# Second attention of a fused block: operand copies within SBUF, reciprocals at a head's last step, output stores ahead of expert weights, normalising on ScalarE

## The reference

```python
x = x + _L0_conv_ref(_gn(x), ...)                   # attention 0: softmax(q k^T * 32**-0.5 + rel_h + rel_w) v, projection
t = t + _L1_attn_ref(_ln_t(t), w_qkv, w_proj, b_proj)   # attention 1: softmax(q k^T / 384**0.5) v, projection
t = t + _L1_ffn_ref(_ln_t(t), ...)                  # top 2 of 8 experts, relu(x w1 + b1) w2 + b2

def _ln_t(v, eps=1e-05):
    m = jnp.mean(v, axis=-1, keepdims=True)
    s = jnp.var(v, axis=-1, keepdims=True)
    return (v - m) / jnp.sqrt(s + eps)
```

## Time and profile before

| | |
|---|---|
| Median of 3 runs (lowest to highest) | 999.45 us (996.57 to 999.99) |
| Profiled execution: its time and its span | 997.88 us, 996.1 us |
| PE, PEld busy | 879.5 us (88%), 675.1 us |
| DVE, ACT, POOL busy | 500.9 us, 353.8 us, 322.3 us |
| Chain of waits, share by engine | PE 41%, issue 7%, DVE 6%, POOL 4%, DMA 4%, SP's queue 4% |
| Attention 0's loop over heads, attention 1's loop | about 123 to 333 us, about 417 to 598 us |
| Closing stages | 339 to 360 us, 604 to 628 us |

### The profile page before, as it was taken

One profiled execution on the slowest core, in us unless ns is written; L12 is line 12 of the kernel. 1 busy time (PEld: TensorE's weight loads), 2 busy tenths in 40 slices (PEclk: granted clock), 3 DMA queues, 4 the chain that ended last, 5 costly groups with the idle time before them and its releaser, 6 DMA issues.

```text
span 996.1 us, 17661 instructions
## 1 busy us (share of the span) xinstructions
PE 879.5 (88%) x6045; PEld 675.1 (68%) x6046; DVE 500.9 (50%) x879; ACT 353.8 (36%) x582; POOL 322.3 (32%) x191
## 2 busy tenths in 40 slices
PE   4969699999999899999999998319999999999991
PEld 3447377677675444666666645319999999999991
DVE  5323666666663344777787725602442442442433
ACT  0112054454545322245455462303342342342330
POOL 0200057677677220166676760140000000000403
PEclk9989699999999999999999999559999999999996
DMA  8474823343334008535555370630652652643214
GB/s 288 96 166 124 289 84 86 100 136 101 106 111 159 13 0 207 142 118 150 191 175 181 121 255 14 232 119 32 238 202 68 245 176 93 230 167 118 87 39 135
DMA packets 77437, 139.21 MB, mean 140 GB/s; under 512 B 14264, under 2 KB 52152, under 8 KB 77392
## 3 DMA queue, kind: packets, MB, share of 16 engines
q1 hardware_dynamic: 66224, 120.62, 39.6%
q10 hardware_dynamic: 9120, 11.74, 3.5%
q0 software_dynamic: 2048, 6.29, 2.0%
HBM read 91.39 MB, written 43.55 MB: 135 GB/s over the span
## 4 chain that ended last, share of the span: by engine, by line
PE 41%; issue 7%; DVE 6%; POOL 4%; DMA 4%; SPq 4%; ACT 1%; ACTq 1%; DVEq 0%; POOLq 0%
PE ps L816 11%; PE ps L805 9%; PE ps L640 6%; PE ps L630 5%; PE ps L619 5%; SPq L362 2%; PE ps L736 2%; POOL xs L569 2%; POOL gy L576 2%; DVE w_lo L1016 1%; DMA xnT<-osb 1%; PE ps L605 1%; DVE mhalf L901 1%; POOL qf L521 1%; DMA heads<-parts 1%
## 5 line engine op out<-in xcount | busy, mean ns | idle before, releaser
L901 DVE TENSOR_REDUCE mhalf<-ps 128x1 f32<-128x512 f32 x384 | 242.5, 679 | 113.6 <-PE ps L619 111.6
L1079 ACT ACTIVATE prob<-ps 128x1024 f32<-128x1024 f32 x192 | 190.4, 1026 | 219.5 <-PE ps L640 95.7
L521 POOL TENSOR_TENSOR qf<-qf,prob 128x1024 f32<-128x1024 f32 x79 | 188.2, 2383 | 16.2 <-POOL qf L521 8.6
L805 PE MATMUL ps<-xT,w 128*128 128x128 f32 x1440 | 165.5, 276 | 1.6 <-issue 1.6
L805 PEld LDWEIGHTS ps<-xT,w 128*128 128x128 f32 x1440 | 164.9, 193 | 2.0 <-issue 2.0
L619 PE MATMUL ps<-km,qm 96*128 96x512 f32 x384 | 149.1, 463 | 7.8 <-DVE mhalf L901 6.8
L630 PE MATMUL ps<-qa,ka 97*128 97x512 f32 x384 | 146.8, 425 | 8.6 <-DMA qa<-row 8.6
L619 PEld LDWEIGHTS ps<-km,qm 96*128 96x128 f32 x384 | 113.3, 320 | 36.1 <-DVE mhalf L901 21.1
L1158 ACT ACTIVATE h_f<-ps,b1c 128x128 f32<-128x128 f32 x240 | 66.9, 377 | 149.0 <-PE ps L805 149.0
L640 PE MATMUL ps<-prob,va 128*32 128x256 f32 x1536 | 107.5, 385 | 0.0
L630 PEld LDWEIGHTS ps<-qa,ka 97*128 97x128 f32 x384 | 69.4, 191 | 54.5 <-issue 27.9
(11 more groups left out here) (128 smaller groups left out, 856.2 us busy)
## 6 DMA issues: line engine op xcount, KB each, us to landing
w<-in_w SPq DMA_DIRECT2D x24, 768.0 KB, 7.3
w_raw<-in_w SPq DMA_DIRECT2D x24, 768.0 KB, 11.9
heads<-parts SPq DMA_DIRECT2D x56, 256.0 KB, 4.6
qa<-heads SPq DMA_DIRECT2D x24, 256.0 KB, 3.6
ka<-heads SPq DMA_DIRECT2D x24, 256.0 KB, 3.7
qb<-heads SPq DMA_DIRECT2D x12, 512.0 KB, 4.5
xs<-zero SPq DMA_DIRECT2D x8, 768.0 KB, 3.8
qm<-heads SPq DMA_DIRECT2D x12, 384.0 KB, 3.7
```

The lines of the kernel that those rows point to most:

```text
L521: pool.tensor_tensor(acc[b], acc[b], prob[:, n % NP, :], ALU.add).then_inc(a_ok[L], 1)
L805: last = mm(ps[:, g, c % HG * P:(c % HG + 1) * P], w1[b][:, k, c * P:(c + 1) * P], xT[:, k, :], start=(k == 0), stop=(k == KT - 1))
L901: v.tensor_reduce(mhalf[:, b, qt, half:half + 1], ps[:, MAX_BANK[i], :], AX.X, ALU.max).then_inc(mx_ok[L], 1)
L1079: act.activation(prob[:, s % NP, :], ps[:, 3 + 2 * (s % 2):5 + 2 * (s % 2), :].rearrange("p a b -> p (a b)"), ACT.Exp).then_inc(p_ok[L], 1)
```

## The change

Five things change.

1. In attention 1, queries and keys are no longer written to DRAM and read back. SP copies them from `parts` to `qm`, `km`, `qa` and `ka`, one part of 32 partitions at a time, so `load_a` has six DMAs where it had four.
2. `invert_sums` runs all four pieces after step 7 of a head (after step 2 of the last head, which has no maxima).
3. In the closing stages ACT makes `tn` from a scale and a shift, DVE makes the shift (one column), the projection has five PSUM banks, and transposes and gate tiles come one step later.
4. `wproj` and the weights of attention 1 are loaded before the loop over heads.
5. Expert 0's weights are loaded after the last output stores, and after the last reads of `parts`.

```diff
@@ SP, per head
+                def held(h, name):
+                    g, m = h
+                    return f(parts[g * HD:(g + 1) * HD, bass.ds(m, 1), PART[name], :].rearrange("p m n -> p (m n)"))
...
                     wait(sp, st_ok[L], TT * (h - 1))
                     sp.sem_inc(a_free, 1)
-                    sp.dma_start(f(qa[b][0:2 * HD, :]), rows(h, "Q_LO", 2)).then_inc(ld_a[L][b], 16)
-                    sp.dma_start(f(qa[b][2 * HD:3 * HD, :]), rows(h, "Q_HI")).then_inc(ld_a[L][b], 16)
-                    sp.dma_start(f(ka[b][0:HD, :]), rows(h, "K_HI")).then_inc(ld_a[L][b], 16)
-                    sp.dma_start(f(ka[b][HD:3 * HD, :]), rows(h, "K_HI", 2)).then_inc(ld_a[L][b], 16)
                     if L == 0:
...
+                    else:
+                        at = at or (h % 4, h // 4)
+                        for i, (query, key) in enumerate((("Q_LO", "K_HI"), ("Q_HI", "K_HI"), ("Q_HI", "K_LO"))):
+                            sp.dma_start(f(qa[b][i * HD:(i + 1) * HD, :]), held(at, query)).then_inc(ld_a[L][b], 16)
+                            sp.dma_start(f(ka[b][i * HD:(i + 1) * HD, :]), held(at, key)).then_inc(ld_a[L][b], 16)
...
-                if L == 1:
+                if L == 0:
+                    for m in range(KT):
+                        store_qk(m)
+                else:
                     sp.wait_ge(pv_ok[0], TT * NH)
-                for m in range(KT):
-                    store_qk(m)
-                    if m == 0 and L == 1:
-                        sp.wait_ge(st_q[1][0], 16 * 8)
-                        first_heads()
+                    sp.wait_ge(split[1], 4)
+                    first_heads()
...
-                sp.wait_ge(st_q[L][1], 16 * 16)
                 load_row(0, 0)
                 load_m(2, 0)
                 load_row(1, 1)
                 load_m(3, 1)
+                if L == 0:
+                    sp.wait_ge(v_mm[0], TT)
+                    load_wqkv(1)
+                else:
+                    sp.wait_ge(pj_mm[0], TT)
+                    sp.wait_ge(split[1], 4 * KT)
+                sp.dma_start(wproj[:], ...).then_inc(ld_p[L], 16)
@@ PE, closing stage
-                        last = mm(ps[:, tt % 4, 0:C], oT[:, k, tt * P:(tt + 1) * P], wproj[:, k, :],
+                        last = mm(ps[:, tt % 5, 0:C], oT[:, k, tt * P:(tt + 1) * P], wproj[:, k, :],
...
-                for tt in range(TT + 3):
+                for tt in range(TT + 4):
                     if tt < TT:
-                        wait(pe, t_ok[L], tt - 3)
-                        project(tt, range(KT) if tt >= 4 else (2,)).then_inc(pj_mm[L], 1)
-                    if 2 <= tt < TT + 2:
-                        turn_stream(tt - 2)
-                    if tt >= 3 and L == 1:
-                        gate_tile(tt - 3)
+                        wait(pe, t_ok[L], tt - 4)
+                        project(tt, range(KT) if tt >= 5 else (2,)).then_inc(pj_mm[L], 1)
+                    if 3 <= tt < TT + 3:
+                        turn_stream(tt - 3)
+                    if tt >= 4 and L == 1:
+                        if tt == 4:
+                            pe.wait_ge(vs_ok[1], NH)
+                        gate_tile(tt - 4)
@@ DVE
-                        if 3 <= s < 7 and not first:
-                            invert_sums(h - 1, s - 3)
+                        if s == (TT - 1 if left else 2) and not first:
+                            for part in range(4):
+                                invert_sums(h - 1, part)
...
                         own(v.reciprocal(rstd[:, tt - 1:tt], sd[:, tt - 1:tt]))
-                        v.tensor_scalar(tn[:, tt - 1, :], t[:, tt - 1, :], mv[:, tt - 1, 0:1], rstd[:, tt - 1:tt],
-                                        ALU.subtract, ALU.mult).then_inc(tn_ok[L], 1)
+                        v.scalar_tensor_tensor(shift[:, tt - 1:tt], mv[:, tt - 1, 0:1], -1.0, rstd[:, tt - 1:tt],
+                                               ALU.mult, ALU.mult).then_inc(norm_ok[L], 1)
@@ ACT, closing stage
+                    if 1 <= tt < TT + 1:
+                        act.wait_ge(norm_ok[L], tt)
+                        act.activation(tn[:, tt - 1, :], t[:, tt - 1, :], ACT.Identity, bias=shift[:, tt - 1:tt],
+                                       scale=rstd[:, tt - 1:tt]).then_inc(tn_ok[L], 1)
```

More of the change, by code:

```diff
@@ L73, in build_program @@
         ps = ctx.enter_context(nc.psum_tensor("ps", [P, 8, HALF], F32))
-        heads_dram = [nc.dram_tensor(f"heads{L}", [NH, len(SLOTS[L]), HD, N], F32).ap() for L in range(2)]
+        heads_dram = nc.dram_tensor("heads", [NH, len(SLOTS), HD, N], F32).ap()
         xs_dram = nc.dram_tensor("xs", [FILLED * P, C], F32).ap()
@@ L250, in build_program @@
         sq_ok = [sem(f"sq_ok{L}") for L in L2]
+        norm_ok = [sem(f"norm_ok{L}") for L in L2]
         t_ok = [sem(f"t_ok{L}") for L in L2]
@@ L371, in load_m @@
+                def load_m(h, b, at=None):
                     wait(sp, sm_ok[L], 2 * TT * (h - 1))
                     sp.sem_inc(m_free, 1)
[L373 to L377, removed]
+                    if L == 0:
+                        sp.dma_start(f(qm[b][:]), rows(h, "Q_HI", 3)).then_inc(ld_m[L][b], 16)
+                        sp.dma_start(f(km[b][0:HD, :]), rows(h, "K_HI")).then_inc(ld_m[L][b], 16)
+                    else:
+                        at = at or (h % 4, h // 4)
+                        sp.dma_start(f(qm[b][0:HD, :]), held(at, "Q_HI")).then_inc(ld_m[L][b], 16)
+                        sp.dma_start(f(km[b][0:HD, :]), held(at, "K_HI")).then_inc(ld_m[L][b], 16)
@@ L444, in _ @@
                 load_m(3, 1)
+                if L == 0:
+                    sp.wait_ge(v_mm[0], TT)
+                    load_wqkv(1)
+                else:
+                    sp.wait_ge(pj_mm[0], TT)
+                    sp.wait_ge(split[1], 4 * KT)
+                sp.dma_start(wproj[:], a[f"wproj{L}"].rearrange("(k p) n -> p k n", p=P)).then_inc(ld_p[L], 16)
                 with sp.Fori(0, (NH - 4) // 4) as q:
@@ L476, in _ @@
                     store_quarter(sp, L, 1, 3, KT - 1, r)
+                if L == 1:
+                    for i in L2:
+                        sp.wait_ge(ld_m[1][i], 32 * NH // 2)
+                        sp.wait_ge(ld_a[1][i], 96 * NH // 2)
+                    load_expert(sp, 0, 0)
             sp.wait_ge(pj_mm[1], TT)
@@ L607, in _ @@
                     last.then_inc(qk_mm[L], 1)
-                n_m, n_a = (2, 5) if L == 0 else (2, 4)
+                n_m, n_a = (2, 5) if L == 0 else (2, 6)
                 kr = 96
@@ L744, in _ @@
                 pe.wait_ge(p_ok[L], TT * NH)
-                for tt in range(4):
+                for tt in range(5):
                     project(tt, (0, 1))
@@ L758, in gate_tile @@
                     for k in range(KT):
-                        last = mm(ps[:, 6, tt * NE:(tt + 1) * NE], xnT[:, k, tt * P:(tt + 1) * P], gate[:, k, :],
+                        last = mm(ps[:, 7, tt * NE:(tt + 1) * NE], xnT[:, k, tt * P:(tt + 1) * P], gate[:, k, :],
                                   start=(k == 0), stop=(k == KT - 1))
@@ L1104, in _ @@
                     store_quarter(act, L, 1, 3, KT - 1, r)
-                for tt in range(TT + 2):
+                for tt in range(TT + 3):
                     if tt < TT:
```

54 lines of the change are left out of this document (28 added, 26 removed).

## The result

The changed kernel takes **1000.6 us** in the median of 11 executions (998.85 to 1004.06), the kernel before 997.82 (11, 994.2 to 999.99): ratio 1.0041, 95% interval 1.0028 to 1.0054. The profiled execution took 998.85 us, its span is 997.0. Timed once more on another chip it took 1000.78 against 997.74, ratio 1.0045 (1.003 to 1.006). All ratios have their 95% interval behind them; they are given as recorded and are not the quotients of the two medians beside them (here 1.0028, and 1.003 the second time). So the difference is +2.8 and +3.0 us by the medians, +3.4 and +3.2 by the means, +4.1 and +4.5 by the ratios.

The account below looks back on a forecast made before the run. PE was taken as the bound, with 41% of the chain of waits. Terms +3.6 + 0.8 - 1.3 + 1.0 - 0.3 = +3.8 us on the profiled 997.88 gave 1001.7, predicted as 1002 us, range 995 to 1009.

Parts of the forecast that it names:

- block in attention 1: Attention 1's loop: four reciprocals in one group start result 10 late, and PE pays in nine heads, +3.6 us (3.2 to 4.7).
- block in attention 0: Attention 0's loop: the four grouped reciprocals delay PE at result 13 in nine heads, +0.8 us (0 to 1.3).
- start of attention 1: First head of attention 1: the row of maxima lands earlier, PE then waits for the last value copy, -1.3 us.
- closing stages: After each attention's heads: `tn` on ACT and the new order cost +1.0 us in attention 1, -0.3 in attention 0.
- moved loads, copies in the loop: Loops over heads: earlier weight loads are free, and a head's six copies, 3.8 us, stay hidden; 0 us.
- clock: Closing stages: another stretch at 1.2 GHz costs up to 1.5 us in attention 1; in attention 0, 1.5 better or worse.
- rival 1: Loops over heads: the grouped reciprocals cost PE nothing, sum -0.6 us, 997.3 us; chance 0.18.
- about 10 us: Attention 1's loop: the sign that L619 on PE would wait for L901 on DVE about 10 us, not 6.8.
- Rival 2: Attention 1's loop: the row of maxima comes late and PE waits in nine heads, +9 us, 1011 us; chance 0.13.
- The 1.4 us wait of the first gate tile: Attention 1's closing stage: PE waits some 1.4 us for the first copy to `xnT`, behind the fourth square root and third `tn`.
- seven short ACT operations: End of attention 1's closing stage: after the last variance at 622.9 they carry the end to 627.2, last gate tile 628.2.
- Rivals 3 and 4: Closing stages: 1.2 GHz once more in each, 1005, chance 0.11; or 2.4 GHz kept and reciprocals free, 994.8, chance 0.08.

Follow-up runs that it names:

- two more issues: Changed kernel with two more copies a head in attention 1's `load_a`, to a DRAM tensor nobody reads: 1004.7 us, ratio 1.0076.
- six more copies: Changed kernel with each of a head's six copies in attention 1's `load_a` issued once more, to a DRAM tensor nobody reads: 1028.0 us, ratio 1.0314.

## Why the prediction was right, point by point

The time and the sign were right: 1002 us forecast, 1000.6 measured, and a sum of +3.8 where the change measured +2.8 to +4.5, by which figure one takes. The base was well chosen too: the sum was added to the profiled execution's 997.88 us, not to the median of three, 999.45, and the median of eleven came to 997.82. The terms did not fit as well as their total (the last row by the pooled means, 3.9 us apart):

| term | forecast | found |
|---|---|---|
| block in attention 1 | +3.6 | +2.6 by the stages; 1.8 to 2.9 at equal clock in five pairs |
| block in attention 0 | +0.8 | 0 to 0.2; the kernel with the block in attention 1 alone is no faster at equal clock |
| start of attention 1 | -1.3 | -1.1 by the stages (79.9 to 78.87 us, old closing stage, without slow stretch), -2.0 at equal clock |
| closing stages | +1.0 and -0.3, together +0.7 | together +0.5 (without the block) and +1.1 (with it) at equal clock |
| moved loads, copies in the loop | 0 | 0.0; no wait inside the loop |
| clock | 0, with up to 1.5 at two places | +2.6 by the fit (0.0034 lower, by 0.76 a thousandth) |

At equal clock the found terms add up to 2.6 + 0.1 - 2.0 + 1.1 = +1.8 and with the clock's 2.6 to +4.4, so they miss the 3.9 by no more than the scatter.

**The block.** The mechanism is shown. It costs where it is moved to, in either kernel; it costs in attention 1 and not in attention 0; and it costs nothing in two halves, whose delay DVE's idle time takes up before result 10. One reading behind it was wrong, though the sum did not use it: no reciprocal stands between results 8 and 9 and result 10 in the kernel before. The one at 491.25 in rows 2 is the head's last, results 8 and 9 are done at about 492.9, and then DVE is idle for 0.86 us. The mis-sized term is attention 1's. I took 0.40 us a head from DVE's lateness at result 10 (0.36 to 0.52). Result 10 starts 1.36 us after PE's pair of scores, at 490.13 against 488.77, where rows 2 had 1.02, so it was 0.34 late, just under the lower bound, and PE paid 0.29 of it. Attention 0's bounds were 0 to 0.15 a head, and the lower one held within the scatter: rows 4 left DVE 1.15 us idle there. So rival 1 is wrong for attention 1 and right for attention 0. My sign of "about 10 us" for L619 was wrong in its view only: the wait of the weight loads grew from 21.1 to 24.7 us.

**Start of attention 1.** As forecast: the row is early, and the last values are next. The equal-clock figure is larger than the stage's by 0.9, about what the scatter allows, and no stage of these profiles shows that part.

**Rival 2** did not happen, but its spare time was small. I had 2.7 us less 1.3, 0.9 and 1.0. In the changed kernel the row's load was issued 3.3 us ahead of its scores in the head of the rows shown (4.35 before), 2.9 in the worst, and two more issues were already too many in one.

**Closing stages.** The 1.4 us wait of the first gate tile came as stepped through, and a like wait at the end, of the fifth tile, which I had folded into "seven short ACT operations". Turning ACT's order round took both away. A `tn` on ACT took 0.706 us (I estimated 0.65). The Trainium skill ("ScalarE: Activation LUTs", section "What ACT_TABLE_LOAD costs") counts 93 ns for each pointer operand over 186 ns and 0.833 ns an element. An estimate by that is 0.692 us here, and the trace agrees to 0.014.

**Rivals 3 and 4, and the clock.** This is the term that made the sum come out. The block is 1.8 us cheaper than forecast over both loops, and by the fit a clock lower by 0.0034 costs 2.6. I had an early stretch at 1.2 GHz in both closing stages as a risk of 0.11. In attention 1's it came in nine of the fourteen profiles, with the old form of the stage too. Three of the five without it have the old form. One such stretch cost about 2.1 us (32.29 against 30.18), where I had up to 1.5. So my forecast was right in part by luck, by two errors of opposite sign.

**What stays open** is why the changed kernel's clock is lower in the mean. Both edits take part: without the block 0.9483, without the new closing stage 0.9506, without both 0.9514, while the block alone lowers the kernel before to 0.9472 in both attentions but to 0.9491, which is hardly lower, in attention 1. The stretches are at the joints between stages (344 to 364, 605 to 618 and 619 to 680, the last two later by as much as the loop is longer with six more copies; with more copies some stand in the loop as well), and kernels with the old form of the stage show each of them. The first is not spread evenly: each of the seven profiles with the new form has one stretch of 3.4 us there, and takes 79.7 to 80.1 us from attention 0's advance projections to attention 1's first scores. Of the seven with the old form five have none and two have two; the two of them that also have the new copies take 78.87 us. So in the changed kernel about 1 us of what the copies save there goes to that stretch again. Why the new form always has it is not shown. The Trainium skill ("TensorE: Matmul & The Clock Gate", section "What's actually happening") says that the gate looks at PE's activity in a rhythm of its own, so that the same kernel has a different number of slow matmuls at its start from run to run. That could give this spread in the middle of a kernel too; no run here shows the rhythm itself. The fit over executions is a statistic, not a mechanism, since some of the slow time lies where PE waits anyway.

## What to carry to other kernels

Small work that is moved together costs nothing until it outgrows the time in which its in-order engine is free ahead of a result that PE waits for (here 1.27 us, against a block of 1.78); look for the smallest such time, and cut the work to fit. When work moves to an in-order engine, write its list so that nobody's copy stands behind a wait for something later. Cut every profile at the same events before believing a difference of 2 us between two: one stretch at the lower clock is as large.

## What was not expected of the hardware

PE's waits were paid about twice where the clock fell among them: with six more copies, attention 1's heads had 14.4 us of waiting, missed 13.6 us of full clock and were 26.9 us longer (210.63 against 183.78). That the waits made the clock fall is likely, since the changed kernel's loop has neither, but no run separates the two. An issue on SP's queue, commonly 0.55 us, took 1.86, 1.97 and 2.05 in three places of the changed kernel's loop, and 1.63 and 2.07 with more copies. The same program's single executions differ by up to 10 us (992.96 to 1003.21), and the granted clock goes with it (0.953 and 0.944).
